# Causal mask of the diagonal row maxima: added by VectorE in the maximum instead of by two TensorE products

## The chip, the cores and the metric

The kernel runs on one core of one Trainium2 chip. The metric is the device time of the whole program in microseconds (us); three runs of it are shown, and their median counts. Differences of about 0.3% are the smallest that such runs tell from nothing.

## What is computed

One transformer block over x of shape (4, 2048, 256) in float32: an adaptive layer norm, causal attention with 16 heads of 16 dimensions, a gated residual, a second adaptive norm, and a mixture of 16 experts (top 4) with one shared expert. The change lies in the attention:

```
q = _apply_rotary(q, rope)
k = _apply_rotary(k, rope)
scores = jnp.einsum('bhqd,bhkd->bhqk', q, k) * scale
causal_mask = jnp.triu(jnp.ones((Tx, Tx), dtype=bool), 1)
scores = jnp.where(causal_mask, -jnp.inf, scores)
attn = jax.nn.softmax(scores, axis=-1)
out = jnp.einsum('bhqk,bhkd->bhqd', attn, v)
```

The softmax needs, for each query row, the largest unmasked score. These maxima are what the change touches.

## The kernel before

**Stages.** Up to about 340 us the prologue norms the input, forms q, k and v in 16 chunks of 512 tokens, rotates them and stores them to HBM in bf16 parts. Then comes the attention, to about 2200 us with its tail; the experts follow. `plan()` writes out one list of named items, and each engine's program walks that list in order and emits its own part of each item. So every engine's queue has the order of the list.

**Groups and steps.** The 64 heads (4 batches x 16) are taken four at a time, which makes 16 groups `g`. The attention of a group is 40 steps `(c, kt)`: `c` is a chunk of 512 queries, `kt` a tile of 128 keys up to the diagonal. A step's width is 512 query columns, but for the last three key tiles of each chunk, which have 384, 256 and 128: 28 full steps and 12 narrow ones in a group. Per step: PE forms the scores of four heads transposed (keys on the partitions), `sa` (L1062), and adds the rows that carry the negated maxima, `sb` (L1075); ACT takes two exponentials of two heads each, `exp` (L1643); in steps on the diagonal GpSimd cuts the triangle of the result (L1797); PE multiplies with the values two steps later, `pv` (L1092). The order on PE within a step is: `pv` of two steps ago, a maximum, `sa` of heads 3 and 2, a maximum, `sa` of the next step's heads 0 and 1, `sb` of heads 3 and 2, a maximum, `sb` of the next step's heads 0 and 1, a maximum. `sa` of the next step's heads 0 and 1 waits until this step's exponential of these heads has read the banks.

**Maxima.** The maxima of group g+1 are taken during the steps of group g, four in a step (16 in the first). An item `("max", g, j, t, kc)` is head `j`, query tile `t` of 128 rows, key chunk `kc` of up to 512 keys. PE forms the scores untransposed (L1039) into one of three PSUM banks (4, 5, 6) that go round; the matmul waits until VectorE has read what lay in its bank. VectorE takes the maximum along the keys (L1460) into `mx`. The widths are n = min(512, 128(t+1) - 512 kc), so the chunk on the diagonal (kc = t // 4) has 128, 256, 384 or 512 columns and all others 512. Of the 80 maxima of a pair of heads in a group, 32 lie on the diagonal; 1024 of 2560 in all. The 160 maxima of group 0 are taken in the second half of the prologue, from banks 1 and 7.

**The mask before.** The last 128 columns of a diagonal chunk need the causal mask. PE adds it in the bank: two further products of bf16 tiles `pick` (rows of the identity) and `tri` (-1e30 above the diagonal), L1042 over 128 columns and L1043 over 64. The second one's completion releases VectorE. `pick` and `tri` are filled at the start of VectorE's program (L1198 to L1204) from the constants.

**Other work of VectorE in the attention.** Reciprocals of the softmax sums (L1494), the output projection's epilogue with the second norm for groups that have one running beside (L1501 to L1530), and, in groups 8 and on, the routing of the first half of the tokens: a chain of some 167 operations (L1229 to L1252 among them), one or two of them in a step.

Of the kernel before, what the change touches and what calls it, by code (L numbers as in the profile page):

```python
# [10 lines left out]
BF16 = mybir.dt.bfloat16  # L11
ALU = mybir.AluOpType
ACT = mybir.ActivationFunctionType
AX = mybir.AxisListType
# [15 lines left out]
BIG = 1e30  # L30
# [431 lines left out]
def program(nc, x, wqk, wv, bqk, bv, wo, ob, gw, gbias, w13, w2, cT, wmod, ropec, ropes, consts, fconst, out):  # L462
# [12 lines left out]
    o, u, jobs = plan()  # L475

    with ExitStack() as ctx:
        s = Sems(nc, ctx)
        PB = ctx.enter_context(nc.psum_tensor("PB", [128, 8, 512], F32))
        A = Arena(nc, (int(nc.sbuf_base) + 31) // 32 * 32)  # L480

        ident = A("ident", [128, 128], F32)
        pick = A("pick", [128, 2, 128], BF16)
        tri = A("tri", [128, 2, 128], BF16)
        mhalf = A("mhalf", [128, 4], F32)
        mT = A("mT", [128, 4, 4], F32)
        obB = A("obB", [128, 256], F32)
# [1 line left out]
        mx = A("mx", [128, 4, 16, 4], F32)  # L489
# [49 lines left out]
        def A_(name, shape, dt, pools=pools):  # L539
            size = (int(np.prod(shape[1:])) * (2 if dt == BF16 else 4) + 31) // 32 * 32  # L540
            pool = next(p for p in [*pools, *late_pools] if p.at + size <= p.end)
            return pool(name, shape, dt)
# [23 lines left out]
        cons = A_("cons", [128, 2, 128], F32)  # L566
# [42 lines left out]
        def nb(step):  # L609

            c, kt = STEPS[step]
            q0 = max(c * 512, kt * 128)
            return (c + 1) * 512 - q0, q0 - c * 512
# [7 lines left out]
        def pbuf(g, i, p):  # L621
            return (2 * (40 * g + i) + p) % NP
# [30 lines left out]
        for name, *at in o.items:  # L653
# [25 lines left out]
            if name == "hs":  # L679
                p, t = at  # L680
# [4 lines left out]
            if name == "scat":  # L685
                p, t, j = at
# [45 lines left out]
        start = o.items.index(("experts",))  # L732
# [221 lines left out]
        def _(pe):  # L954
            q = Once(pe)
# [15 lines left out]
            for name, *at in o.items:  # L971
                item = (name, *at)
                if name == "mod":
                    q.wait_ge(s["l_wm"], 16)
                    q.wait_ge(s["c_v"], 3)
                    for n, (kind, f) in enumerate([(k, f) for k in (0, 1) for f in (0, 1)]):
                        for k in (0, 1):
                            col = kind * 256 + f * 128
                            mm = pe.matmul(PB[:, 7, 4 * n:4 * n + 4], wm_s[:, k, col:col + 128], sc[:, k, :], start=k == 0, stop=k == 1)
                    mm.then_inc(s["m_mod"], 1)  # L980
                elif name == "turn":
# [5 lines left out]
                    for i in range(4):  # L987
                        mm = pe.transpose(PB[:, 0, 128 * i:128 * i + 128], xn[:, c % 2, i, 128 * f:128 * f + 128], ident[:, :])
                    mm.then_inc(s["tp"], 1)
                elif name == "gates":  # L990
                    for n, kind in enumerate((2, 5, 3, 4)):
                        for k in (0, 1):
                            mm = pe.matmul(PB[0:4, 1 + 5 * (n // 2), 256 * (n % 2):256 * (n % 2) + 256], sc[:, k, :],
                                           wm_s[:, k, kind * 256:kind * 256 + 256], start=k == 0, stop=k == 1)
# [4 lines left out]
                    for k in (0, 1):  # L999
                        mm = pe.matmul(PB[:, 7, 256:512], bvB[:, k, :], wo_s[:, k, :], start=k == 0, stop=k == 1)  # L1000
                    mm.then_inc(s["m_bv"], 1)
                elif name == "qk":
# [6 lines left out]
                    mm = pe.matmul(PB[:, 2 + m, :], wqk_s[:, f, 128 * m:128 * m + 128], hT[:, c % 2, f, :], start=f == 0, stop=f == 1)  # L1009
                    if f == 1:  # L1010
                        mm.then_inc(s["qk"], 1)
                elif name == "v":
# [6 lines left out]
                    for f in (0, 1):  # L1019
                        mm = pe.matmul(PB[:, 6, 256 * (i % 2):256 * (i % 2) + 256], hT[:, c % 2, f, 128 * i:128 * i + 128],  # L1020
                                       wv_s[:, f, :], start=f == 0, stop=f == 1)
# [9 lines left out]
                elif name == "max":  # L1031
                    g, j, t, kc = at
                    k3, n = (g + 2) % 3, min(512, 128 * (t + 1) - 512 * kc)
                    bank = u.bank[item]
                    q.wait_ge(s[f"l_g{k3}"], 16 * NL * (g // 3 + 1))
                    if item in freed:
                        q.wait_ge(*freed[item])
                    half = slice(64 * (j % 2), 64 * (j % 2) + 64)
                    mm = pe.matmul(PB[:, bank, 0:n], QO[half, k3, j, 128 * t:128 * t + 128], KO[half, k3, j, 512 * kc:512 * kc + n],  # L1039
                                   start=True, stop=True)  # L1040
                    if kc == t // 4:
                        pe.matmul(PB[:, bank, n - 128:n], pick[half, 0, :], tri[half, 0, :], start=False, stop=True, skip_group_check=True)  # L1042
                        mm = pe.matmul(PB[:, bank, n - 64:n], pick[half, 1, :], tri[half, 1, 64:128], start=False, stop=True,  # L1043
                                       skip_group_check=True)
                    mm.then_inc(s["max"], 1)
                elif name == "nturn":
                    g, p = at
# [4 lines left out]
                elif name == "sa":  # L1052
                    g, i, j = at
                    c, kt = STEPS[i]
                    k3, p = (g + 2) % 3, j // 2
                    n, c0 = nb(i)
# [3 lines left out]
                    if o.n("exp", g, i, p) > 2:  # L1060
                        q.wait_ge(s["exp"], o.n("exp", g, i, p) - 2)
                    pe.matmul(PB[:, j, 0:n], KO[rows, k3, j, 128 * kt:128 * kt + 128], QO[rows, k3, j, q0:q0 + n],  # L1062
                              start=True, stop=False).then_inc(s["sa"], 1)
                elif name == "sb":
                    g, i, j = at
                    c, kt = STEPS[i]
                    k3, p = (g + 2) % 3, j // 2
                    n, c0 = nb(i)
# [4 lines left out]
                    if g:  # L1073
                        q.wait_ge(s["l_att"], 112)
                    pe.matmul(PB[:, j, 0:n], KO[rows, k3, j, 128 * kt:128 * kt + 128], QO[rows, k3, j, q0:q0 + n],  # L1075
                              start=False, stop=True).then_inc(s["st"], 1)
                elif name == "pv":
                    g, i = at
                    c, kt = STEPS[i]
                    n, c0 = nb(i)  # L1080
# [10 lines left out]
                    for j in range(4):  # L1091
                        mm = pe.matmul(PB[32 * j:32 * j + 17, 7, c0:512], V[:, g % 2, kt, 17 * j:17 * j + 17],  # L1092
                                       P[:, pbuf(g, i, j // 2), j % 2, 0:n], start=kt == 0, stop=True, skip_group_check=True)
                    mm.then_inc(s["pv"], 1)
                elif name == "o_proj":
                    b, t = at
                    bank = u.bank[item]
# [7 lines left out]
                    for k in (0, 1):  # L1105
                        mm = pe.matmul(PB[:, bank, 0:256], ON[:, k, 128 * t:128 * t + 128], wo_s[:, k, :], start=k == 0, stop=k == 1)  # L1106
                    mm.then_inc(s["proj"], 1)
                elif name == "o_turn":
                    b, t = at
                    i, bank = 16 * b + t, u.bank[item]  # L1110
# [5 lines left out]
                    for f in (0, 1):  # L1116
                        mm = pe.transpose(PB[:, bank, 128 * f:128 * f + 128], h2t[:, i % 3, 128 * f:128 * f + 128], ident[:, :])
                    mm.then_inc(s["o_turn"], 1)
                elif name == "o_logits":
                    b, t = at  # L1120
                    i, bank = 16 * b + t, u.bank[item]
# [6 lines left out]
                    for f in (0, 1):  # L1128
                        mm = pe.matmul(PB[:, bank, 0:16], lT[:, f, :], gw_s[:, f, :], start=f == 0, stop=f == 1)  # L1129
                    mm.then_inc(s["logits"], 1)  # L1130
                elif name == "cnt":
# [3 lines left out]
                    if item in after:  # L1135
                        for wait in banks_free[u.bank[item]]:
# [3 lines left out]
                              start=True, stop=True).then_inc(s["cnt"], 1)  # L1140
                elif name == "jin":
# [7 lines left out]
                    for f in (0, 1):  # L1149
                        mm = pe.transpose(PB[:, k, 128 * f:128 * f + 128], xq[n % XQ][:, 128 * f:128 * f + 128], ident[:, :])  # L1150
                    mm.then_inc(s["jt"], 1)
                elif name == "jgate":
# [9 lines left out]
                    for m in range(3):  # L1162
                        for f in (0, 1):
                            w = ws[:, k, f] if kind == "x" else W13[:, f, E]
                            mm = pe.matmul(PB[:, 2 + k, 128 * m:128 * m + 128], w[:, 128 * m:128 * m + 128], xT[:, k, f, :],  # L1165
                                           start=f == 0, stop=f == 1)
                    mm.then_inc(s["gu"], 1)
                elif name == "jdown":
# [10 lines left out]
                    for f in (0, 1):  # L1179
                        w = W2[f][:, expert(n), :] if kind == "x" else W2S[f][:, i // 16, :]  # L1180
                        mm = pe.matmul(PB[:, bank, 0:256], haT[:, k, f, :], w, start=f == 0, stop=f == 1)  # L1181
# [3 lines left out]
        def _(dve):  # L1185
            q = Once(dve)
# [7 lines left out]
            dve.tensor_copy(ident[:, :], cons[:, 0, :]).then_inc(s["c_k"], 1)  # L1194
            dve.memset(mx[:, :, :, :], -3.0e38).then_inc(s["c_k"], 1)
            dve.memset(mhalf[:, :], -0.5).then_inc(s["c_k"], 1)
            dve.memset(pick[:, :, :], 0.0).then_inc(s["c_k"], 1)
            dve.memset(tri[64:128, 0, 64:128], -BIG).then_inc(s["c_k"], 1)  # L1198
            q.wait_ge(s["c_k"], 4)
            for lo, v, cols in ((0, 0, 0), (0, 1, 64), (64, 0, 0), (64, 1, 64)):  # L1200
                half = slice(lo, lo + 64)
                dve.tensor_copy(pick[half, v, cols:cols + 64], cons[half, 0, lo:lo + 64]).then_inc(s["c_k"], 1)
                dve.tensor_copy(tri[half, v, cols:cols + 64], cons[half, 1, lo:lo + 64]).then_inc(s["c_k"], 1)
            dve.tensor_copy(tri[0:64, 0, 64:128], cons[0:64, 1, 64:128]).then_inc(s["c_k"], 1)  # L1204

            step = [0]

# [180 lines left out]
            for name, *at in o.items:  # L1388
                item = (name, *at)
# [45 lines left out]
                elif name == "rot":  # L1435
                    c, z, half = at
# [3 lines left out]
                    lo, hi = 2 + 2 * z, 3 + 2 * z  # L1440
                    q.wait_ge(s["qk"], 4 * c + 2 * z + 1)
                    q.wait_ge(s["l_w"], 80)
                    n = 4 * c + 2 * z + half - 1
# [12 lines left out]
                elif name == "max":  # L1456
                    g, j, t, kc = at
                    n = min(512, 128 * (t + 1) - 512 * kc)
                    q.wait_ge(s["max"], o.n(*item))
                    dve.tensor_reduce(mx[:, j, t, kc:kc + 1], PB[:, u.bank[item], 0:n], AX.X, ALU.max).then_inc(s["mx"], 1)  # L1460
                elif name == "neg":
                    g, p = at
                    q.wait_ge(s["mx"], max_n(g, 2 * p + 1))
# [3 lines left out]
                elif name == "nturn":  # L1467
                    g, p = at
                    bank, n = u.bank[item], o.n(*item)
# [17 lines left out]
                elif name == "inv":  # L1487
                    b, gi, c = at
                    n = 4 * (4 * b + gi) + c
# [5 lines left out]
                elif name == "o_proj":  # L1495
                    b, t = at
# [5 lines left out]
                elif name == "o_stat":  # L1502
                    b, t = at
# [12 lines left out]
                elif name == "o_h2":  # L1516
                    b, t = at
# [8 lines left out]
                elif name == "o_logits":  # L1526
                    b, t = at
# [17 lines left out]
                elif name == "comb":  # L1545
                    p, t, j = at
                    i, k, n = FIRST[p] + t, t % YG, o.n(*item)
# [6 lines left out]
                elif name == "gated":  # L1554
                    p, t = at
# [3 lines left out]
                elif name == "res":  # L1559
                    p, t = at  # L1560
# [364 lines left out]
```

## Time and profile before

| | us |
|---|---|
| median of three runs | 3058.89 |
| lowest, highest | 3057.62, 3067.77 |
| span of the profiled execution (first to last instruction) | 3061.1 |

For the profiled execution its span is what is known; it is 2.2 us above the median of the runs and lies within their spread.

The page names engines PE (TensorE matmul), PEld (its weight loads), DVE (VectorE), ACT (ScalarE), POOL (GpSimd) and SP (SyncE). A matmul's end is modelled, and matmuls run into each other in the pipeline, so the sum of their busy times is more than the time they take of the engine. The chain that ended last is followed back from the last instruction to what released each step. Stretches are given in us from the start of the span. The mean granted TensorE clock of the run is 0.978 of full speed.

### The profile page before, as it was taken

To read this page: it belongs to the slowest core of one execution; us is meant where nothing else is said; L and a number is where in the kernel's file an instruction comes from. 1 tells how busy PE (TensorE), PEld (TensorE's weight loads), DVE (VectorE), ACT (ScalarE), POOL (GpSimd) and SP (SyncE) were. 2 spreads that over 40 slices of the span, in tenths; PEclk is the share of its full clock that TensorE was granted. 3 is DMA by queue.
4 is the path that set the end of the run, shared out by engine and by line. 5 is a ranking of instruction groups with operands and counts; after the bars stand their busy time and mean duration, and the time that the engine had idled before them with its cause. 6 is when DMAs were issued, how large, how long until landed. Compare 5 with 4: busy or idle time off the path is not lost.

```text
span 3061.1 us, 61038 instructions
## 1 busy us (share of the span) xinstructions
PE 2843.4 (93%) x22500; PEld 1573.9 (51%) x22500; DVE 2242.9 (73%) x5047; ACT 1779.3 (58%) x2736; POOL 1253.7 (41%) x1557
## 2 busy tenths in 40 slices
PE   7888799999999999989999999987999999999997
PEld 4433333333433334433333333323888999999997
DVE  7888788888888888899998888822393225566477
ACT  2422466666566665656665566665556666666533
POOL 6766311213521114521114765554305753443176
PEclk9999899999999999999999999998999999999998
DMA  4854323313312322412323535245336765665486
GB/s 163 209 142 106 110 56 65 66 42 76 101 39 56 66 63 59 109 43 37 66 63 91 141 94 123 89 129 152 117 93 204 233 202 175 187 183 173 136 238 193
DMA packets 290690, 359.05 MB, mean 117 GB/s; under 512 B 65404, under 2 KB 243212, under 8 KB 290140
## 3 DMA queue, kind: packets, MB, share of 16 engines
q1 hardware_dynamic: 259516, 279.94, 33.8%
q0 software_dynamic: 26112, 71.34, 7.7%
q10 hardware_dynamic: 4768, 3.88, 0.5%
q8 instruction: 182, 2.98, 0.4%
q14 instruction: 112, 0.92, 0.1%
HBM read 206.25 MB, written 139.21 MB: 113 GB/s over the span
## 4 chain that ended last, share of the span: by engine, by line
PE 49%; ACT 13%; DVE 10%; POOL 7%; issue 7%; DMA 2%; ACTq 1%; POOLq 0%; SPq 0%; DVEq 0%
ACT P L1643 13%; PE PB L1165 10%; PE PB L1092 8%; PE PB L1181 7%; DVE mx L1460 6%; PE PB L1062 6%; PE PB L1039 6%; PE PB L1075 5%; POOL x_slots L1846 4%; PE PB L1106 2%; PE PB L1150 2%; ACTq L1652 1%; POOL yg L1859 1%; PE PB L1129 1%; POOL x_slots L1838 1%
## 5 line engine op out<-in xcount | busy, mean ns | idle before, releaser
L1460 DVE TENSOR_REDUCE mx<-PB 128x1 f32<-128x512 f32 (+3 forms) x2560 | 1406.9, 603 | 214.6 <-PE PB L1039 135.6
L1643 ACT ACTIVATE P<-PB 128x1024 f32<-128x1024 f32 (+3 forms) x1280 | 1095.4, 894 | 643.3 <-PE PB L1075 629.3
L1039 PE MATMUL PB<-KO,QO 64*128 64x512 bf16 (+3 forms) x2560 | 762.0, 353 | 61.5 <-DVE mx L1460 51.5
L1092 PE MATMUL PB<-P,V 128*17 128x512 f32 (+3 forms) x5120 | 599.2, 540 | 11.8 <-POOL P L1797 11.7
L1062 PE MATMUL PB<-QO,KO 64*128 64x512 bf16 (+3 forms) x2560 | 546.8, 353 | 60.0 <-ACT P L1643 33.0
L1039 PEld LDWEIGHTS PB<-KO,QO 64*128 64x128 bf16 x2560 | 203.5, 94 | 718.0 <-DVE mx L1460 533.0
L1075 PE MATMUL PB<-QO,KO 34*128 34x512 bf16 (+3 forms) x2560 | 520.0, 351 | 0.6 <-DMA QO<-nh 0.4
L1797 POOL TENSOR_SCALAR_AFFINE_SELECT P<-P 128x256 f32<-128x256 f32 x512 | 208.6, 414 | 678.8 <-ACT P L1643 673.1
L1165 PE MATMUL PB<-xT,ws 128*128 128x128 f32 x3432 | 433.7, 277 | 7.1 <-ACT xT L1726 7.0
L1165 PEld LDWEIGHTS PB<-xT,ws 128*128 128x128 f32 x3432 | 408.2, 193 | 9.7 <-ACT xT L1726 9.7
L1571 DVE TENSOR_TENSOR haT<-sl,PB 64x128 f32<-64x128 f32 x350 | 101.4, 290 | 411.8 <-ACT sl L1735 407.3
L1859 POOL DMA_INDIRECT yg<-y_slots,sidu x256 | 249.6, 975 | 302.5 <-DVE acc L1552 118.9
L1181 PE MATMUL PB<-W,haT 128*128 x1144 | 298.3, 384 | 12.1 <-DVE haT L1572 8.3
L1062 PEld LDWEIGHTS PB<-QO,KO 64*128 64x128 bf16 x2560 | 150.6, 94 | 253.6 <-ACT P L1643 224.9
L1735 ACT ACTIVATE sl<-PB 128x256 f32<-128x256 f32 x350 | 134.2, 383 | 250.8 <-PE PB L1165 248.1
L1719 ACT ACTIVATE ws<-W 128x768 f32 x286 | 239.6, 838 | 25.9 <-issue 25.9
L1075 PEld LDWEIGHTS PB<-QO,KO 34*128 34x128 bf16 x2560 | 185.1, 94 | 92.2 <-PE PB L1062 32.0
L1042 PE MATMUL PB<-tri,pick 64*128 64x128 bf16 x1024 | 214.8, 217 | 0.0
L1181 PEld LDWEIGHTS PB<-W,haT 128*128 128x128 f32 x1144 | 196.3, 191 | 31.5 <-issue 16.0
L1846 POOL DMA_INDIRECT x_slots<-Rsg,sidu x172 | 166.9, 970 | 84.0 <-ACT P L1643 47.7
L1043 PE MATMUL PB<-tri,pick 64*128 64x64 bf16 x1024 | 190.2, 190 | 0.0
L1804 POOL TENSOR_TENSOR osb<-osb,rden 128x512 f32<-128x512 f32 x64 | 82.8, 1294 | 239.5 <-DMA rden<-rden_rows 235.2
(178 smaller groups left out, 3218.7 us busy)
## 6 DMA issues: line engine op xcount, KB each, us to landing
xq<-x_slots SPq DMA_DIRECT2D x286, 128.0 KB, 2.8
qk_parts<-pt SPq DMA_DIRECT2D x192, 128.0 KB, 2.4
KO<-qk_parts SPq DMA_DIRECT2D x192, 128.0 KB, 4.1
y_slots<-yo SPq DMA_DIRECT2D x191, 128.0 KB
QO<-qk_parts SPq DMA_DIRECT2D x64, 256.0 KB, 3.4
rden<-rden_rows SPq DMA_DIRECT2D x256, 64.0 KB
y_slots<-mx SPq DMA_DIRECT2D x95, 128.0 KB
v_rows<-vst SPq DMA_DIRECT2D x16, 544.0 KB, 4.0
```

The costliest lines, as they stand in the source:

```text
L1039: mm = pe.matmul(PB[:, bank, 0:n], QO[half, k3, j, 128 * t:128 * t + 128], KO[half, k3, j, 512 * kc:512 * kc + n], start=True, stop=True)
L1042: pe.matmul(PB[:, bank, n - 128:n], pick[half, 0, :], tri[half, 0, :], start=False, stop=True, skip_group_check=True)
L1062: pe.matmul(PB[:, j, 0:n], KO[rows, k3, j, 128 * kt:128 * kt + 128], QO[rows, k3, j, q0:q0 + n], start=True, stop=False).then_inc(s["sa"], 1)
L1075: pe.matmul(PB[:, j, 0:n], KO[rows, k3, j, 128 * kt:128 * kt + 128], QO[rows, k3, j, q0:q0 + n], start=False, stop=True).then_inc(s["st"], 1)
L1092: mm = pe.matmul(PB[32 * j:32 * j + 17, 7, c0:512], V[:, g % 2, kt, 17 * j:17 * j + 17], P[:, pbuf(g, i, j // 2), j % 2, 0:n], start=kt == ...
L1165: mm = pe.matmul(PB[:, 2 + k, 128 * m:128 * m + 128], w[:, 128 * m:128 * m + 128], xT[:, k, f, :], start=f == 0, stop=f == 1)
L1181: mm = pe.matmul(PB[:, bank, 0:256], haT[:, k, f, :], w, start=f == 0, stop=f == 1)
L1460: dve.tensor_reduce(mx[:, j, t, kc:kc + 1], PB[:, u.bank[item], 0:n], AX.X, ALU.max).then_inc(s["mx"], 1)
L1643: act.activation(P[:, pbuf(g, i, p), :, 0:n], PB[:, 2 * p:2 * p + 2, 0:n], ACT.Exp, scale=0.25).then_inc(s["exp"], 1)
L1719: act.activation(ws[:, k], W13[:, :, bass.ds(of[p, i], 1), :].rearrange("p f o c -> p f (o c)"), ACT.Copy).then_inc(s["ws"], 1)
L1846: pool.indirect_dma_start(xg_d[p][:, :], bass.IndirectOffsetOnAxis(sidu[:, i, j:j + 1], 0), hs[k], None).then_inc(s[f"w_s{p}{k}"], 16)
L1859: pool.indirect_dma_start(yg[:, k, j, :], None, y_d[p][:, :], bass.IndirectOffsetOnAxis(sidu[:, i, j:j + 1], 0)).then_inc(s[f"l_yg{k}"], 16)
```

## The change

For a maximum on the diagonal, the two triangle products on PE go; the first product alone releases VectorE. VectorE's `tensor_reduce` becomes, for these maxima only, a `tensor_tensor_reduce`: it adds the last n columns of a bf16 mask `mk` (384 columns of zeros, then the triangle of -1e30) to the n scores in PSUM, writes the sums back to the same place, and gives their maximum, begun at -3e38, as a second output to `mx`. `mk` takes the place of `pick` and `tri` and is filled by one fill and one copy; VectorE then waits for its first five constants. The waits on semaphores, the order of the list and the banks are as before.

```diff
--- before.py
+++ after.py
@@ -480,8 +480,7 @@
         A = Arena(nc, (int(nc.sbuf_base) + 31) // 32 * 32)
 
         ident = A("ident", [128, 128], F32)
-        pick = A("pick", [128, 2, 128], BF16)
-        tri = A("tri", [128, 2, 128], BF16)
+        mk = A("mk", [128, 512], BF16)
         mhalf = A("mhalf", [128, 4], F32)
         mT = A("mT", [128, 4, 4], F32)
         obB = A("obB", [128, 256], F32)
@@ -1038,10 +1037,6 @@
                     half = slice(64 * (j % 2), 64 * (j % 2) + 64)
                     mm = pe.matmul(PB[:, bank, 0:n], QO[half, k3, j, 128 * t:128 * t + 128], KO[half, k3, j, 512 * kc:512 * kc + n],
                                    start=True, stop=True)
-                    if kc == t // 4:
-                        pe.matmul(PB[:, bank, n - 128:n], pick[half, 0, :], tri[half, 0, :], start=False, stop=True, skip_group_check=True)
-                        mm = pe.matmul(PB[:, bank, n - 64:n], pick[half, 1, :], tri[half, 1, 64:128], start=False, stop=True,
-                                       skip_group_check=True)
                     mm.then_inc(s["max"], 1)
                 elif name == "nturn":
                     g, p = at
@@ -1194,14 +1189,9 @@
             dve.tensor_copy(ident[:, :], cons[:, 0, :]).then_inc(s["c_k"], 1)
             dve.memset(mx[:, :, :, :], -3.0e38).then_inc(s["c_k"], 1)
             dve.memset(mhalf[:, :], -0.5).then_inc(s["c_k"], 1)
-            dve.memset(pick[:, :, :], 0.0).then_inc(s["c_k"], 1)
-            dve.memset(tri[64:128, 0, 64:128], -BIG).then_inc(s["c_k"], 1)
-            q.wait_ge(s["c_k"], 4)
-            for lo, v, cols in ((0, 0, 0), (0, 1, 64), (64, 0, 0), (64, 1, 64)):
-                half = slice(lo, lo + 64)
-                dve.tensor_copy(pick[half, v, cols:cols + 64], cons[half, 0, lo:lo + 64]).then_inc(s["c_k"], 1)
-                dve.tensor_copy(tri[half, v, cols:cols + 64], cons[half, 1, lo:lo + 64]).then_inc(s["c_k"], 1)
-            dve.tensor_copy(tri[0:64, 0, 64:128], cons[0:64, 1, 64:128]).then_inc(s["c_k"], 1)
+            dve.memset(mk[:, 0:384], 0.0).then_inc(s["c_k"], 1)
+            dve.tensor_copy(mk[:, 384:512], cons[:, 1, :]).then_inc(s["c_k"], 1)
+            q.wait_ge(s["c_k"], 5)
 
             step = [0]
 
@@ -1457,7 +1447,11 @@
                     g, j, t, kc = at
                     n = min(512, 128 * (t + 1) - 512 * kc)
                     q.wait_ge(s["max"], o.n(*item))
-                    dve.tensor_reduce(mx[:, j, t, kc:kc + 1], PB[:, u.bank[item], 0:n], AX.X, ALU.max).then_inc(s["mx"], 1)
+                    if kc == t // 4:
+                        dve.tensor_tensor_reduce(PB[:, u.bank[item], 0:n], PB[:, u.bank[item], 0:n], mk[:, 512 - n:512], 1.0, -3.0e38,
+                                                 ALU.add, ALU.max, mx[:, j, t, kc:kc + 1]).then_inc(s["mx"], 1)
+                    else:
+                        dve.tensor_reduce(mx[:, j, t, kc:kc + 1], PB[:, u.bank[item], 0:n], AX.X, ALU.max).then_inc(s["mx"], 1)
                 elif name == "neg":
                     g, p = at
                     q.wait_ge(s["mx"], max_n(g, 2 * p + 1))
```

## Rows read from the trace of the kernel before

**Rows 1.** The page, part 1: busy us (share of span) xinstructions

```profile
PE 2843.4 (93%) x22500; PEld 1573.9 (51%) x22500; DVE 2242.9 (73%) x5047; ACT 1779.3 (58%) x2736; POOL 1253.7 (41%) x1557
```

**Rows 2.** Stretches: us, PE, PEld, DVE, ACT, POOL busy, PEclk; then L1460's DVE alone

```profile
140.00:340.00 200.00, 162.70 (x598) 67.04 (x597) 161.78 (x314) 56.47 (x65) 116.72 (x57) 0.90 0.52 139
340.00:2010.00 1670.00, 1587.07 (x14387) 592.85 (x14387) 1463.36 (x3004) 1065.04 (x1304) 549.39 (x897) 0.99 0.30 74
1200.00:1600.00 400.00, 376.42 (x3357) 140.80 (x3353) 372.47 (x799) 246.18 (x307) 106.94 (x191) 1.00 0.26 61
...
340.00:2010.00 1670.00, 1316.57 (x2400) 0.99 0.30 74
1200.00:1600.00 400.00, 305.35 (x556) 1.00 0.26 61
```

**Rows 3.** Chain by line: 560:640, then 400:2010, then 1200:1600

```profile
by line: ACT P L1643 36.0%; PE PB L1092 14.9%; PE PB L1062 13.2%; PE PB L1039 11.0%; PE PB L1075 10.1%; issue 8.5%; DVE mx L1460 5.7%; PE PB L1043 0.8%; PE PB L1042 0.7%; PE PB L1050 0.3%
...
by line: ACT P L1643 21.6%; PE PB L1092 14.2%; DVE mx L1460 11.1%; PE PB L1039 10.8%; PE PB L1062 10.1%; PE PB L1075 9.1%; issue 7.7%; PE PB L1106 2.7%; ACTq L1652 1.9%; PE PB L1129 1.2%; PE PB L1043 0.8%; PE PB L1042 0.7%; PE PB L1117 0.6%
...
by line: DVE mx L1460 27.6%; PE PB L1092 13.2%; ACT P L1643 10.4%; PE PB L1039 10.3%; PE PB L1075 7.3%; PE PB L1062 7.2%; issue 5.4%; PE PB L1106 2.1%; ACTq L1652 1.6%; PE PB L1129 1.6%; DVE Rcm L1229 1.2%; DVE Rsb L1240 1.1%; DVE Rsa L1229
```

**Rows 4.** Chain pieces of 560:640: start us, us, what

```profile
588.66 1.95 ACT P L1643 x2
...
591.33 1.95 ACT P L1643 x2
```

**Rows 5.** Timeline 575.5:584: start us, us, operation [idle before]

```profile
575.88 2.48 DVE L1460 TENSOR_REDUCE mx<-PB 128x1 f32<-128x512 f32 x4 [0.24 <-PE PB L1039]
...
576.73 0.38 PE L1039 MATMUL PB<-KO,QO 64*128 64x512 bf16 x1
```

**Rows 6.** Chain pieces of 1400:1470, routing between maxima

```profile
1402.29 0.56 DVE Rrk L1240
...
1403.45 2.39 DVE mx L1460 x4
```

**Rows 7.** Triangle products: their groups (page), then chain pieces of 1400:1470

```profile
L1042 PE MATMUL PB<-tri,pick 64*128 64x128 bf16 x1024 | 214.8, 217 | 0.0
...
L1043 PE MATMUL PB<-tri,pick 64*128 64x64 bf16 x1024 | 190.2, 190 | 0.0
...
1442.53 0.06 PE PB L1042
1442.59 0.03 PE PB L1043
```

**Rows 8.** Reductions of L1460: page group, then by form

```profile
L1460 DVE TENSOR_REDUCE mx<-PB 128x1 f32<-128x512 f32 (+3 forms) x2560 | 1406.9, 603 | 214.6 <-PE PB L1039 135.6
...
L1460 DVE TENSOR_REDUCE mx<-PB 128x1 f32<-128x512 f32 x1792 | 1130.9, 684 | 148.5 <-PE PB L1039 135.6 <-PE PB L1043 2.2
...
L1460 DVE TENSOR_REDUCE mx<-PB 128x1 f32<-128x256 f32 x256 | 98.9, 416 | 13.0 <-PE PB L1043 11.1
...
L1460 DVE TENSOR_REDUCE mx<-PB 128x1 f32<-128x128 f32 x256 | 62.5, 281 | 14.3 <-PE PB L1043 13.8
```

**Rows 9.** Other VectorE work: groups by form, then timeline 30:48 and 0:22

```profile
L1501 DVE TENSOR_TENSOR xo<-PB,obB 128x256 f32<-128x256 f32 x64 | 27.1, 423 | 58.7 <-PE PB L1106 58.4
...
L1515 DVE TENSOR_SCALAR vef<-mvf 128x1 f32<-128x1 f32 x64 | 9.8, 154 | 2.2
...
31.20 0.73 DVE L1449 SCALAR_TENSOR_TENSOR tb<-PB,bqk_s,rS 128x512 f32<-128x512 f32 x1
31.86 0.73 DVE L1446 SCALAR_TENSOR_TENSOR ta<-PB,bqk_s,rS 128x512 f32<-128x512 f32 x1
...
12.80 0.38 DVE L1398 BATCH_NORM_AGGREGATE mv<-st 128x2 f32<-128x6 f32 x4
```

**Rows 10.** Timeline 0:22: the fill and last cast that go

```profile
10.06 0.11 DVE L1198 MEMSET tri<- 64x64 bf16 x1
...
11.27 0.19 DVE L1204 CAST tri<-cons 64x64 bf16<-64x64 f32 x1
```

## Prediction

> **What bounds the kernel now.** I read the page first: VectorE is busy 73% of the span and PE 93% [rows 1], but the change touches only the part in which maxima are taken. That part is found with the stretches: 2400 of the 2560 maxima lie in 340 to 2010 us, the other 160 in 140 to 340 us [rows 2]. In 340 to 2010 VectorE is busy 1463 of 1670 us, so it has 207 us of idle time in all; in 1200 to 1600, where the routing of the first half also runs on it, it is busy 372.5 of 400 [rows 2]. A shares-of-busy reading would say "PE 95%, DVE 88%, both nearly full" and stop. The chain that ended last says more. In 560 to 640 it runs through ACT (36%) and through PE's score and value products, and only 5.7% through the maxima; over 400 to 2010 the maxima hold 11.1%, the two triangle products 0.8% + 0.7%; in 1200 to 1600 the maxima hold 27.6% [rows 3].
>
> The pieces show why. In a step with 512 query columns the chain is a loop: two exponentials in 1.95 us, then L1062 and L1075, then the next two; from 588.66 to 591.33 that is 2.67 us [rows 4]. The PE queue makes this loop: the score products of the next step wait for the first exponential and stand ahead of the mask-row products that the second one needs. Beside it VectorE takes four maxima in 2.48 us and then idles 0.24 [rows 5]. So in such a step VectorE has about 0.24 us of slack and PE's triangle products lie beside the exponentials. Of 40 steps in a group 28 are full; in the 12 narrow ones the exponentials shrink (three quarters to one quarter of the width) while four maxima stay to be taken, and PE or VectorE ends last. In 1200 to 1600 the chain alternates between maxima (four in 2.39 us) and routing operations (0.56) [rows 6]: there VectorE bounds.
>
> **What goes from PE.** L1042 and L1043 are 1024 each, 214.8 + 190.2 = 405 us of busy time, but matmuls are pipelined: on the chain a pair costs 0.06 + 0.03 us [rows 7], so the pairs are worth at most 1024 x 0.09 = 92 us of PE. On the chain of 400 to 2010 they hold 1.5% of 1610 = 24 us [rows 3]. This is what their removal can give at first order. What comes late next is the ACT loop or a maximum, so I keep two thirds: -16 us. In the routing stretch they hide under VectorE and give nothing.
>
> **What comes to VectorE.** 1024 of the 2560 reductions (40%: 32 of 80 in each pair of heads) become an add with a maximum, which reads PSUM and a bf16 tile, writes the sum back to the bank, and writes the maximum to a second output. The trace of before has no such operation. Reductions of 128, 256 and 512 columns last 281, 416 and 684 ns, those of 384 in the middle of the last two [rows 8]. Three bounds for the added time per instruction:
> - Low: nothing. A two-input tensor_tensor over PSUM of 256 columns (L1501) lasts 423 ns against 416 for the reduction [rows 8, 9]; if the second output comes with the stream, the difference is +0.01.
> - Middle: the second output is a small instruction of its own. The smallest that stand back to back are the aggregations: four in 0.38 us, the last of them about as long as a one-column operation, 0.154, so (0.38 - 0.154) / 3 = 0.075 apart [rows 9].
> - High: the main part like scalar_tensor_tensor (512 columns start to start 0.66 [rows 9], against 0.60 for reductions, from (2.48 - 0.684) / 3 of [rows 5]: +0.06) and a read that costs a whole small operation, 0.154 [rows 9]: +0.22 rounded up.
> I take +0.105: the middle read, 0.075, and half of the way (0.03) from the tensor_tensor row to the scalar_tensor_tensor row, since this operation has two tensor inputs as well as two constants. Both ends stay for the range. Below nothing is excluded: every element still streams once.
>
> The Trainium skill, "VectorE: DVE Perf Modes", section "Two Vector instructions with no wait between them", says that an operation that also writes out its accumulator is two instructions, the main one and an accumulator read. No run here shows it. By it the low bound falls away and the sum below would be no lower than with 0.075.
>
> **The sum.**
> - Stretch 1200 to 1600: 556 maxima [rows 2], 40% = 222, x 0.105 = 23 us more on an engine with 27.5 us idle. The chain passes VectorE in at least 30% of this stretch and alternates at the scale of a few us [rows 3, 6]; I let half through: +12.
> - Rest of 400 to 2010: maxima on the chain are 11.1% of 1610 minus 27.6% of 400 = 179 - 110 = 69 us; at 0.55 us each (1406.9 / 2560 [rows 8]) 125 instructions, 40% = 50, x 0.105 = +5. The full steps swallow theirs: at most two of their four maxima are masked (or four of 128 and 256 columns, which are short anyway), 0.21 against 0.24 of slack.
> - 140 to 340, group 0: 64 masked maxima, +6.7 on VectorE (busy 162 of 200) and -5.8 on PE (busy 163) [rows 2]. Neither is full; take +1.
> - Start: nine casts and a fill between 10.06 and 11.46 us become one cast and one fill [rows 10], -1.
> - PE: -16.
> Together +1 us. The profiled span is 3061.1, 2.2 above the median 3058.9 and inside the three runs (3057.6 to 3067.8); I add the sum to the median: 3060.
>
> **Waits and queues.** The release of a bank now stands behind the read of the maximum. Behind it on PE waits the product of the third-next maximum (three banks), and behind that all of PE's queue. In a full step a first maximum starts at 575.88 and ends by 576.5, while the product that wants its bank starts at 576.73 [rows 5]: 0.2 us to spare, which +0.105 leaves open and +0.22 closes.
>
> **The rivals.**
> 1. Relief without a price (+0.01 per instruction): +1 in the routing stretch, 0 elsewhere, -24 on PE, -1 at the start: 3035 to 3040. For it: tensor_tensor's row. Against: the second output.
> 2. The products go, but nothing was waiting for them: PE gives 0, the price stands: +12 + 5 + 1 - 1 = +17, 3076. For it: the ACT loop of 2.67 us, in which they do not appear.
> 3. VectorE becomes the bound. It decides from 0.12 per instruction on, where two masked maxima eat the slack of 0.24 [rows 5]. At +0.22: 222 x 0.22 = 49 less half of the 27.5 idle = +35; narrow steps, where by plan()'s order 10 masked maxima of a group of 64 meet a step that VectorE bounds, x the 11 groups outside the routing stretch x 0.22 = +24 (27 rounded down for what was idle); three full steps per group with two 512-wide masked ones, 0.44 - 0.24 = 0.2, x 33 = +7; group 0 +11; PE -12: +65, 3124.
> 4. Half rate: the added input or output makes the masked maxima stream at half the speed. Each gains its streaming time again, 281 to 684 ns less about 150, mean 0.33 us [rows 8], x 1024 = 340 us on an engine with 207 idle: above 3200. Against it: the two-input operations of the trace run at full rate [rows 9]. The Trainium skill, "Vector Engine (DVE) Microarchitecture Reference", section "Points that are easy to get wrong", gives such a halving for two non-bf16 SBUF sources; here one source is PSUM and the other bf16, and no run here shows that layout.
>
> **How the numbers follow.** Forecast (3051 to 3068) 0.38, rival 1 0.27, rival 2 0.18, rival 3 0.13, rival 4 0.04. About 0.3% (9 us) is what a measurement here can tell from no change. Faster: rival 1 and a little of the forecast's low side, 0.28. Slower: rivals 2 to 4, 0.35. Same: 0.37. Range 3034 to 3100: it holds rivals 1 and 2 and the lower half of rival 3 (0.12 to 0.17 per instruction); above it lie the rest and rival 4.
>
> **What the changed profile would show.** L1042/L1043 gone, PE's instructions down by 4096 (matmuls and weight loads), its share of the span nearly as before. The masked group's mean against 281, 416, 684: if it is more by 0.1 and a second small row stands beside it, the price is right. Full steps still 2.67 us apart on the chain with ACT in them; narrow steps shorter by up to 0.2. 1200 to 1600 stretched by 10 to 15 us with VectorE at 95% or more. I am wrong if full steps are longer than 2.67 (price above 0.12), or if the chain's share of maxima in 560 to 640 rises well over 5.7%.

## The result

| | us |
|---|---|
| before, median of 9 runs | 3061.87 |
| changed kernel, median of 9 runs | 3048.64 (3046.22 to 3058.43) |
| ratio, with its 95% interval | 0.9964 (0.9952 to 0.9976) |
| span of the profiled execution, before and changed | 3061.1 and 3054.9 |

The change makes the kernel 0.36% faster, about 11 us (0.0036 x 3062; the two medians are 13 us apart). The prediction was 3060 and no change. Its range (3034 to 3100) holds the time; its sum, +1 us, does not hold the sign.

First the page of the changed kernel, part 1, against [rows 1]: engine, busy us (share of span), xinstructions.

```profile
PE 2811.3 (92%) x20452; PEld 1453.5 (48%) x20452; DVE 2282.0 (75%) x6062; ACT 1780.3 (58%) x2736; POOL 1252.3 (41%) x1557
```

PE lost 2048 matmuls and 2048 weight loads but only 32 us of busy time where the products' groups had added up to 405 us: those busy times lay over one another. VectorE gained 39 us and 1015 instructions: 1024 for the second output, less the nine fills and casts by which the start got shorter. The stretches of the changed kernel, against [rows 2] (us; busy PE, PEld, DVE, ACT, POOL; granted clock):

```profile
340.00:2010.00 1670.00, 1558.20 (x12500) 478.06 (x12500) 1504.19 (x3969) 1068.20 (x1308) 551.11 (x903) 0.98 0.30 75
1200.00:1600.00 400.00, 370.43 (x2879) 114.88 (x2877) 376.72 (x1008) 244.68 (x304) 103.45 (x186) 0.97 0.26 61
```

VectorE rose from 1463 to 1504 us in the attention and only from 372.5 to 376.7 in the routing stretch. The groups of the masked maxima, by form, against [rows 8]:

```profile
L1451 DVE CUSTOM_DVE_ANT_0 PB<-PB,mk 128x512 f32<-128x512 f32 x256 | 172.0, 712 | 1.8 <-PE PB L1038 1.2
L1451 DVE DVE_READ_ACCUMULATOR2_ANT mx<- 128x1 f32 x1024 | 142.9, 140 | 0.0
L1451 DVE CUSTOM_DVE_ANT_0 PB<-PB,mk 128x384 f32<-128x384 f32 x256 | 138.3, 579 | 30.7 <-PE PB L1038 29.4
L1451 DVE CUSTOM_DVE_ANT_0 PB<-PB,mk 128x256 f32<-128x256 f32 x256 | 104.9, 439 | 5.9 <-PE PB L1038 5.9
L1451 DVE CUSTOM_DVE_ANT_0 PB<-PB,mk 128x128 f32<-128x128 f32 x256 | 69.2, 308 | 12.6 <-PE PB L1038 12.3
```

The operation is two instructions: the add with its running maximum (308, 439, 579, 712 ns, 23 to 28 above the reductions) and a read of the accumulator, 140 ns. Adding 28 and 140 would give a price of 0.17 us, and that would be wrong, as the order in time shows (timeline of the changed kernel, VectorE; start us, us):

```profile
503.19 0.73 DVE L1451 CUSTOM_DVE_ANT_0 PB<-PB,mk 128x512 f32<-128x512 f32 x1
503.84 0.14 DVE L1451 DVE_READ_ACCUMULATOR2_ANT mx<- 128x1 f32 x1
503.84 0.73 DVE L1451 CUSTOM_DVE_ANT_0 PB<-PB,mk 128x512 f32<-128x512 f32 x1
504.49 0.14 DVE L1451 DVE_READ_ACCUMULATOR2_ANT mx<- 128x1 f32 x1
```

The read and the next operation start together, at 503.84, and from there to the next start it is 0.65 us, against 0.60 for reductions. This pair is not the usual one, though: here the first of the two masked maxima itself starts together with the read of the one before it. The usual pair stands behind a plain reduction:

```profile
513.70 0.69 DVE L1451 CUSTOM_DVE_ANT_0 PB<-PB,mk 128x512 f32<-128x512 f32 x1
514.31 0.14 DVE L1451 DVE_READ_ACCUMULATOR2_ANT mx<- 128x1 f32 x1
514.31 0.73 DVE L1451 CUSTOM_DVE_ANT_0 PB<-PB,mk 128x512 f32<-128x512 f32 x1
514.96 0.14 DVE L1451 DVE_READ_ACCUMULATOR2_ANT mx<- 128x1 f32 x1
```

Its first one takes 0.61 from start to start (513.70 to 514.31) and only its second one 0.65 (514.31 to 514.96). So a masked maximum costs 0.01 us more than a reduction where it stands free, and 0.05 more where it starts together with the read of another; the medians of the narrower ones say the same (256 columns: 0.34 and 0.38 against 0.33). Of the 1024 masked maxima in this trace 489 start together with a read. On the mean that is (489 x 0.05 + 535 x 0.01) / 1024 = 0.03 us, less than a third of the 0.105 that the prediction took. The chain by line of 560 to 640, against [rows 3]:

```profile
by line: ACT P L1637 38.6%; PE PB L1057 12.5%; PE PB L1087 11.2%; PE PB L1070 9.8%; PE PB L1038 9.2%; issue 9.1%; DVE mx L1454 7.3%; DVE PB L1451 1.5%; ACTq L1646 0.7%; PE PB L1045 0.3%; DVE mx L1451 0.1%
```

PE's lines shrank (values 14.9 to 11.2%, scores of the maxima 11.0 to 9.2%), ACT grew from 36.0 to 38.6%, and the maxima from 5.7 to 8.9% (7.3 + 1.5 + 0.1).

### The profile page after: what moved, and what is told of

Same layout as the page of the kernel before. It is cut to its first block, busy times and chain, and to the rows that moved or that the text cites. A ratio compares the mean times of both kernels' runs of the same rounds, so it can differ in the third digit from the quotient of the medians.

```text
span 3054.9 us, 57958 instructions
## 1 busy us (share of the span) xinstructions
PE 2811.3 (92%) x20452; PEld 1453.5 (48%) x20452; DVE 2282.0 (75%) x6062; ACT 1780.3 (58%) x2736; POOL 1252.3 (41%) x1557
## 3 DMA queue, kind: packets, MB, share of 16 engines
q8 instruction: 166, 2.72, 0.4%
## 4 chain that ended last, share of the span: by engine, by line
PE 44%; DVE 13%; ACT 13%; issue 7%; POOL 7%; DMA 2%; ACTq 1%; SPq 1%; POOLq 0%; DVEq 0%
ACT P L1637 13%; PE PB L1160 11%; PE PB L1176 7%; PE PB L1087 6%; DVE mx L1454 6%; PE PB L1057 5%; PE PB L1038 5%; PE PB L1070 5%; POOL x_slots L1840 4%; DVE PB L1451 2%; PE PB L1101 2%; PE PB L1145 2%; ACTq L1646 1%; PE PB L1124 1%; POOL x_slots L1832 1%
## 5 line engine op out<-in xcount | busy, mean ns | idle before, releaser
L1454 DVE TENSOR_REDUCE mx<-PB 128x1 f32<-128x512 f32 x1536 | 975.8, 682 | 122.3 <-PE PB L1038 114.8
L1451 DVE CUSTOM_DVE_ANT_0 PB<-PB,mk 128x128 f32<-128x128 f32 (+3 forms) x1024 | 481.4, 509 | 51.0 <-PE PB L1038 48.8
L1070 PE MATMUL PB<-QO,KO 34*128 34x512 bf16 (+3 forms) x2560 | 502.4, 352 | 1.0 <-DMA QO<-nh 0.9
L1160 PEld LDWEIGHTS PB<-xT,ws 128*128 128x128 f32 x3432 | 409.5, 193 | 10.4 <-ACT xT L1720 10.2
L1057 PEld LDWEIGHTS PB<-QO,KO 64*128 64x128 bf16 x2560 | 137.2, 94 | 273.1 <-ACT P L1637 242.4
L1070 PEld LDWEIGHTS PB<-QO,KO 34*128 34x128 bf16 x2560 | 163.1, 94 | 98.0 <-PE PB L1057 32.9
L1087 PEld LDWEIGHTS PB<-P,V 128*17 128x17 f32 x5120 | 85.3, 95 | 183.9 <-issue 157.7
```

Source lines behind the costliest of these rows:

```text
L1451: dve.tensor_tensor_reduce(PB[:, u.bank[item], 0:n], PB[:, u.bank[item], 0:n], mk[:, 512 - n:512], 1.0, -3.0e38, ALU.add, ALU.max, mx[:, j ...
```

## The experiments

Theory A after the result: the relief of PE is what was forecast, 16 us, and the price was taken twice too high. Its 0.05 us was read from the first pair above alone; the mean of 0.03 was not known when the expectations were written. Theory B: the price is right in total and the relief is larger. Both explain -11, so relief and price were taken apart. The first four kernels shared one chip, with 22 runs of the kernel before (median 3062.6); the last two shared 17 (median 3061.5).

**The changed kernel again** (no edit).

> The changed kernel again, on the chip of the other three runs, so that they have one base. Theory A (the relief of PE is about as forecast, -16 us, but the price of a masked maximum is 0.05 us and not 0.105: 0.65 against 0.60 start to start for 512 columns): -9 us against before, ratio 0.997. Theory B (the price is as forecast in total, and the relief of PE is larger, 24 us or more): the same -9, told apart only by the next two.

Measured: ratio 0.9963 (0.9950 to 0.9976), -11.3 us.

**The relief alone.** Plain reductions for all maxima, no products:

```diff
-                    if kc == t // 4:
-                        dve.tensor_tensor_reduce(PB[:, u.bank[item], 0:n], PB[:, u.bank[item], 0:n], mk[:, 512 - n:512], 1.0, -3.0e38,
-                                                 ALU.add, ALU.max, mx[:, j, t, kc:kc + 1]).then_inc(s["mx"], 1)
-                    else:
-                        dve.tensor_reduce(mx[:, j, t, kc:kc + 1], PB[:, u.bank[item], 0:n], AX.X, ALU.max).then_inc(s["mx"], 1)
+                    dve.tensor_reduce(mx[:, j, t, kc:kc + 1], PB[:, u.bank[item], 0:n], AX.X, ALU.max).then_inc(s["mx"], 1)
```

> The changed kernel with plain reductions for all maxima: the triangle products are gone and nothing is added on VectorE. The causal mask is left out of the maxima on the diagonal (the softmax is then shifted by a maximum that may be too large). It gives the relief of PE alone. Theory A: -16 to -18 us against before (ratio 0.9945). Theory B: -25 us or more (0.992). If the products were hidden anyway: 0.

Measured: ratio 0.9945 (0.9923 to 0.9967), -16.8 us. That is theory A's number; B's 25 us lies outside the interval, but narrowly (0.9923 would be 23.6), and "hidden anyway" lies far outside.

**The price alone.** Both masks, one on each engine. To make room, `pick`, `tri` and `mk` share one tile `W` (zeros, identity, zeros, triangle, -1e30); the products' sizes stay:

```diff
-        pick = A("pick", [128, 2, 128], BF16)
-        tri = A("tri", [128, 2, 128], BF16)
+        W = A("W", [128, 704], BF16)
...
+                        at = 512 + 64 * (j % 2)
+                        pe.matmul(PB[:, bank, n - 128:n], W[half, 64:192], W[half, at:at + 128], start=False, stop=True, skip_group_check=True)
+                        mm = pe.matmul(PB[:, bank, n - 64:n], W[half, 0:128], W[half, at:at + 64], start=False, stop=True,
...
+                    if kc == t // 4:
+                        dve.tensor_tensor_reduce(PB[:, u.bank[item], 0:n], PB[:, u.bank[item], 0:n], W[:, 640 - n:640], 1.0, -3.0e38,
```

> The kernel before with its two products kept and the fused add and maximum on VectorE as well: the mask is added twice. It gives the price alone. Theory A (0.05 us per masked maximum): 11 in the routing stretch x half = +5.5, +2.5 in the rest, +0 to +2 in the prologue: +8 us, ratio 1.0026. Theory B (0.105 in effect): +17, ratio 1.0055.

Measured: ratio 1.0018 (1.0006 to 1.0029), +5.5 us. The forecast's +17 (1.0055) is outside the interval, so theory B falls here. Relief and price add up: -16.8 + 5.5 = -11.3, the time of the changed kernel. That they do so to the last digit is luck: the interval of the relief alone is 13 us wide.

**Split by stretch.** Against the kernel of the price alone:

```diff
+KEEP = (10, 11, 12)
...
-                    if kc == t // 4:
+                    if kc == t // 4 and g in KEEP:
...
-                    if kc == t // 4:
+                    if kc == t // 4 and g not in KEEP:
```

> Groups 10, 11 and 12, whose maxima meet the routing on VectorE, keep the products on PE and the plain reduction; all other groups have the change. Theory A with the loss in the routing stretch: 4 to 6 us faster than the changed kernel (ratio to before 0.9950), half groups of 54 us in the routing stretch as before. If the routing stretch loses nothing by the change: as the changed kernel.

Measured: ratio 0.9951 (0.9932 to 0.9969), -15 us. The times alone do not tell it from the changed kernel (the intervals overlap by most of their width). The traces do, where it counts: the five half groups of the routing stretch take 271.9 us before, 274.2 in the changed kernel and 272.1 here. So the stretch loses 2.3 us by the change and the split gives 2.1 of them back; the 4 to 6 us of the expectation are not shown. These are single traces, and they can be compared because none of the three has time at the lower clock in the stretch. How closely such traces agree is seen in the five half groups one by one, where the split kernel does the same work as the kernel before: 54.04, 54.43, 53.92, 54.20, 55.50 against 54.04, 54.43, 53.75, 54.19, 55.49. The first trace of the changed kernel has 10.2 us at the lower clock there and takes 276.5.

**One and two more small operations** before each masked maximum:

```diff
+                        for _ in range(2):
+                            if more[0] >= 16:
+                                q.wait_ge(s["more"], more[0] - 15)
+                            z = more[0] % 16
+                            dve.tensor_copy(junk[:, z:z + 1], mhalf[:, 0:1]).then_inc(s["more"], 1)
+                            more[0] += 1
```

> The changed kernel with one more one-column copy on VectorE before each masked maximum (1024 in all, about 0.07 to 0.1 us each by the small operations of the trace), so that a masked maximum costs some 0.12 to 0.15 more than the plain reduction: the size that the prediction took, and the point from which rival 3 was said to decide. If the slack of 0.24 us in a full step holds as the prediction put it (little passes below the point): half groups of 48.77 and 52.07 us grow by 0.1 to 0.3, routing ones by 1; in total 6 to 10 us above the changed kernel, ratio to before 0.999. If all of the added time passes in half groups: 32 x 0.1 = 3.2 us in each.

Measured: ratio 1.0015 (1.0005 to 1.0025), +4.6 us, so about 16 us above the changed kernel (0.0052 x 3062) where 6 to 10 were expected. The half groups of 48.77 and 52.07 grew by 0.2 and 0.1, as expected; those of the routing stretch by 1.4 each, with 10.2 us at the lower clock in this trace and none in the changed kernel's.

> The same with two copies before each masked maximum, 0.2 to 0.25 us above the plain reduction, the upper bound of the prediction. If there is a point near 0.12 from which VectorE decides, the second copy costs clearly more than the first: half groups 1 to 2 us longer, routing ones 2 or more, in total 30 us or more above the changed kernel (ratio to before 1.006 to 1.02). If no such point lies below 0.25: twice the first copy's cost.

Measured: ratio 1.0071 (1.0057 to 1.0084), +21.7 us. The second copy adds 17 us to the 16 of the first, which is the expectation without a point. Its timeline on VectorE (start us, us):

```profile
513.44 0.69 DVE L1458 CUSTOM_DVE_ANT_0 PB<-PB,mk 128x512 f32<-128x512 f32 x1
514.05 0.14 DVE L1458 DVE_READ_ACCUMULATOR2_ANT mx<- 128x1 f32 x1
514.05 0.21 DVE L1456 COPY junk<-mhalf 128x1 f32<-128x1 f32 x2
514.18 0.70 DVE L1458 CUSTOM_DVE_ANT_0 PB<-PB,mk 128x512 f32<-128x512 f32 x1
```

From 513.44 to 514.18 it is 0.74: a masked maximum with its copies stands 0.14 above a plain reduction. With one copy the same distance is 0.67, 0.07 above, so that kernel did not reach the 0.12 to 0.15 that it was built for. A copy stands between every read and the next masked maximum here, and the masked ones of 512 columns last 0.69 again. So a price beyond the point of 0.12 makes the kernel slower, as rival 3 said, by a third of the 65 us that it was given.

**Where the time goes, step by step.** The time between two `nm` reductions is half a group (20 steps); the time from a step's first exponential to the next step's is a step. All in us, from one trace of each kernel ("changed" is the one run again); the half groups end at the `nm` reductions number 28 and 29, counted from 0, the routing stretch has half groups 20 to 24, and the steps are those of group 5 that differ anywhere by more than 0.03:

| | before | changed | relief alone | price alone | one more | two more |
|---|---|---|---|---|---|---|
| half group 28 | 49.28 | 48.79 | 48.59 | 49.41 | 49.01 | 49.53 |
| half group 29 | 52.53 | 52.05 | 51.98 | 52.65 | 52.14 | 52.31 |
| routing stretch (5 half groups) | 271.9 | 274.2 | 272.0 | 274.9 | 281.3 | 287.7 |
| of it at the lower clock | 0 | 0 | 6.8 | 0 | 10.2 | 10.2 |
| group 5, 40 steps | 101.81 | 100.84 | 100.54 | 102.03 | 101.16 | 101.85 |
| full step 0 | 2.62 | 2.62 | 2.62 | 2.62 | 2.62 | 2.69 |
| steps 2, 10, 11, 22 (narrow), sum | 8.18 | 7.76 | 7.76 | 8.18 | 7.76 | 7.87 |
| steps 3 and 23 (narrow), each | 2.24 | 2.36 | 2.24 | 2.36 | 2.44 | 2.58 |
| steps 4 and 24 (full), sum | 5.71 | 5.43 | 5.54 | 5.60 | 5.44 | 5.43 |
| step 18 (full, four masked) | 2.91 | 2.67 | 2.67 | 2.91 | 2.67 | 2.72 |
| step 19 (full, after it) | 3.10 | 3.01 | 3.01 | 3.10 | 3.01 | 3.01 |
| step 37 (narrow, four masked) | 2.08 | 2.08 | 2.08 | 2.08 | 2.21 | 2.40 |
| steps 38 and 39 (narrow), sum | 4.98 | 4.79 | 4.64 | 5.05 | 4.81 | 4.81 |

The other 26 steps are the same to 0.03 in all six kernels; 19 of them are full steps of 2.67. Two experiments' ACT rows show such steps, first the changed kernel (run again), then the one with two copies more (timeline, ACT; start us, us, [idle before]):

```profile
929.13 1.94 ACT L1637 ACTIVATE P<-PB 128x1024 f32<-128x1024 f32 x2 [0.73 <-PE PB L1070]
931.80 1.94 ACT L1637 ACTIVATE P<-PB 128x1024 f32<-128x1024 f32 x2 [0.73 <-PE PB L1070]
934.47 1.02 ACT L1637 ACTIVATE P<-PB 128x1024 f32<-128x1024 f32 x1 [0.73 <-PE PB L1070]
```

```profile
593.63 1.94 ACT L1644 ACTIVATE P<-PB 128x1024 f32<-128x1024 f32 x2 [0.73 <-PE PB L1071]
596.30 1.94 ACT L1644 ACTIVATE P<-PB 128x1024 f32<-128x1024 f32 x2 [0.73 <-PE PB L1071]
598.97 1.94 ACT L1644 ACTIVATE P<-PB 128x1024 f32<-128x1024 f32 x2 [0.73 <-PE PB L1071]
```

2.67 us in both, with the same 0.73 of idle time. The kernel before has the same loop but loses it where four of the maxima are masked (timeline, ACT):

```profile
938.10 1.94 ACT L1643 ACTIVATE P<-PB 128x1024 f32<-128x1024 f32 x2 [0.73 <-PE PB L1075]
941.01 1.02 ACT L1643 ACTIVATE P<-PB 128x1024 f32<-128x1024 f32 x1 [0.97 <-PE PB L1075]
```

941.01 - 938.10 = 2.91: in step 18, whose four masked maxima of 384 and 512 columns put eight triangle products into PE's queue, the mask-row products come 0.24 later (0.97 of idle time against 0.73). In the changed kernel the same step is 934.47 - 931.80 = 2.67. Eight products are not enough by themselves: step 17, with four masked maxima of 128 and 256 columns, takes 2.67 in both. Which of the products of step 18 delay it was not separated.

## Why the prediction was wrong, point by point

- **The step that failed is the price of a masked maximum.** "I take +0.105: the middle read, 0.075, and half of the way (0.03)". Measured, start to start: 0.05 where the masked maximum starts together with another's read (0.65 against 0.60 for 512 columns, 0.52 against 0.47 for 384), 0.01 where it stands free (0.61, 0.48), 0.03 on the mean. The low bound (+0.01) and the middle (0.075) enclose it. There is a read, as the Trainium skill says ("VectorE: DVE Perf Modes", section "Two Vector instructions with no wait between them"; the trace agrees, 1024 reads of 140 ns), but the next operation starts with it. I took the distance of two small operations for what one small operation adds behind a long one. In whole runs the forecast put the price at 12 + 5 = 17 us, and the price alone measured 5.5.
- **The share that passes in the routing stretch** was forecast as half. The 160 masked maxima of the five half groups add 160 x 0.03 = 5 us on VectorE. Price alone against before, both without time at the lower clock there, gives 274.9 - 271.9 = 3.0; changed against relief alone gives 274.2 - 272.0 = 2.2, where the relief's trace has 6.8 us at the lower clock. That is about half, by single traces: no second error is shown.
- **The relief came out as forecast, in part by luck.** -16 forecast as two thirds of the products' 24 us on the chain, -16.8 measured (-10 to -24). But the prediction has no term for the clock, and the kernels without the products ran at a lower mean granted clock (last section): at the same clock the relief would be about -22 by my estimate. Where it lands was only half right, too. Narrow steps give 0.42 + 0.34 us of the 1.27 per group, as said. The rest is in full steps that I had written off: steps 18, 19, 4 and 24 (0.24 + 0.09 + 0.17). "At most two of their four maxima are masked (or four of 128 and 256 columns, which are short anyway)" overlooked step 18, which has four of 384 and 512.
- **The rest of the sum.** +5 was forecast for the chain outside the routing stretch, 1.5 with 0.03 (50 x 0.03); in group 5 the price is 0.22 (102.03 - 101.81), over the 11 groups that the prediction counts outside the stretch 2.4.
- **The sum again:** with 0.03 in place of 0.105, and nothing else touched, it is 3.3 (222 x 0.03, half of it) + 1.5 - 16 + 1 - 1 = -11 us, inside the interval's -7 to -15. One term of the right kind and the wrong size turned a small gain into none. That it meets -11 so closely is chance: the clock has no term in it, and the others were rounded.
- **The ACT loop held:** full steps 2.67 in every kernel, with up to 0.14 us more per masked maximum, but for steps 0 and 18 (0.08 and 0.05 longer with two copies). The expected "maxima's share of the chain well over 5.7%" did come (8.9%) without a longer full step; as a sign of being wrong it was badly chosen, since a shorter chain raises every share that stays.
- **Rival 1** (relief without a price, 3035 to 3040) had the sign and too much of it; the relief kernel, which is that case, measured -16.8; the rival's -24 lies just outside its interval, and by the estimate at the same clock (-22) it is not far off. **Rival 2** falls with the relief kernel. **Rival 3:** its point is not one. The full steps with two masked maxima of 512 columns, where the slack of 0.24 was to be used up, are steps 8, 16, 28 and 36 (the prediction counts three); with two copies each they carry 2 x 0.14 = 0.28 and stay at 2.62 or 2.67. From 0.03 to 0.07 per masked maximum group 5 grows by 0.32 us and from 0.07 to 0.14 by 0.69, mostly in steps 3, 23 and 37 and without a break; the routing stretch takes 13.5 us of the 33 us between the changed kernel and that with two copies (0.0108 x 3062). **Rival 4:** 512 columns last 712 against 684 ns, and the last 128 of them add 133 ns in both (712 - 579, 684 - 551): the rate is that of the reductions.
- **The start and group 0** cannot be read to a microsecond: the second `nm` reduction comes at 330.3 us before, at 334.3 and 331.4 in the two traces of the changed kernel, and at 333.1 with the relief alone.

The split version is the fastest here whose maxima are masked, by its median ratio (0.9951 against 0.9963), but not by more than the intervals leave open. Leaving the mask out of the maxima altogether (0.9945) is only as good as the scores: where a masked score lies far above all unmasked ones, the exponentials vanish.

## What to carry to other kernels

Price an added instruction by start-to-start distances of the very pairing that the change makes (a small one behind a long one), not by its own duration and not by a row of small ones: 140 ns of duration cost 10 to 50 here, by what stood before. Look at more than one pair: the first that I read gave the upper of two values. When an engine's share is high, look step by step at which loop sets the pace; an edit between two engines that are each "nearly full" can pay on one and be free on the other, in different steps. And where two guessed terms of opposite sign nearly cancel, say so in the chances: the sign hangs on the less certain one.

## What the runs showed of the hardware

**Two costs of one instruction.** A masked maximum that starts together with the accumulator read of another lasts longer: 0.73 us instead of 0.69 for 512 columns, 0.65 instead of 0.61 from start to start. With a copy of one column in between it is 0.69 again, and a plain reduction that starts together with a read shows no such addition (0.60 to the next start). Why this is so the runs do not show.

**The granted clock.** PE's granted clock was lower in the prologue than in the attention. In 140 to 340 us it was 0.90 before, with PE busy 163 of 200 us, against 0.99 in 340 to 2010, with PE busy 95% [rows 2], and in the changed kernel, run again:

```profile
140.00:340.00 200.00, 161.50 (x472) 61.15 (x472) 163.86 (x376) 56.47 (x65) 116.31 (x56) 0.88 0.52 139
```

Up to 340 us the time at the lower of the two levels (1.2 GHz) was 46.5 us before and 53.4 with the price alone, both with the products; without them 59.8 and 59.2 (changed, two traces), 59.5 (relief), 53.5 and 58.6 (one and two copies more), and 52.3 in the split version. These are single traces. The whole runs say more, as each has its mean granted clock:

| kernel | runs | mean of the granted clock |
|---|---|---|
| before, on the two chips of the experiments | 22 and 17 | 0.9775 and 0.9776 |
| price alone (products kept) | 11 | 0.9776 |
| split (products kept in three groups) | 5 | 0.9770 |
| changed, result and run again | 9 and 9 | 0.9751 and 0.9761 |
| relief alone | 8 | 0.9744 |
| one and two copies more (no products) | 12 and 6 | 0.9743 and 0.9745 |

The kernels without the products ran at a clock lower by 0.0014 to 0.0034. Among the runs of one kernel, 0.001 less of clock goes with 1.3 to 2.2 us more of time (0.9 in the split version, 1.8 over all). So about 3 to 6 us of what the removal gives went back through the clock; this is an estimate from these runs, and no experiment changed the clock alone. The price alone and the kernel before ran at the same clock, so its +5.5 us has no such part.

In the attention the stretches at the lower level come singly, most of them 3.4 or 6.8 us long, in other places in each run: with one of 3.4 us at 505 us a half group of the kernel before takes 54.83 instead of 52.55 us. This is why half groups and steps were compared and not only totals.
